# Cross attention: four PSUM banks shared in one ring, and quadrant swaps written as a maximum

## The reference, cut to what matters

```
q = (query @ Wq + bq).reshape(B, L, NKV, G, HDIM)      # 512 -> 32 heads of 128
k_, v_ = split(kv @ Wkv + bkv, 2, axis=-1)             # 512 -> 8 + 8 heads of 128
scores = einsum('blkgd,bmkd->bkglm', q, k) * scale
attn = softmax(scores, axis=-1)
o = einsum('bkglm,bmkd->blkgd', attn, v).reshape(B, L, NHEAD * HDIM)
return o @ Wo + bo
x = _layernorm(x + that)
```

## Time and profile before

| | |
|---|---|
| three runs | 2900.38 us median (2898.84 to 2906.28) |
| the profiled execution | 2909.86 us, its span on the core 2908.0 us |
| busy over the span | PE 2756.5 (95%), PEld 2389.1 (82%), DVE 1962.4 (67%), ACT 1461.6 (50%), POOL 1595.9 (55%) |
| chain that ended last | PE 84%, DVE 10%, issue 2%, POOL 2%, ACT 2%, DMA 1% |
| mean granted clock of TensorE | 0.984 |
| first scores of cross attention read by DVE | 1651.82 us |
| scores of step 60 read by DVE | 2750.49 us |

### The profile page before, as it was taken

The page is one execution under the profiler, slowest core; times in us unless marked ns, Lnnn a source line. Parts: engine busy times, 40 slices in busy tenths (PEclk is TensorE's granted clock), DMA queues, the critical chain, the costliest instruction groups (busy, mean ns, idle before and its releaser), DMA issues.

```text
span 2908.0 us, 63698 instructions
## 1 busy us (share of the span) xinstructions
PE 2756.5 (95%) x26368; PEld 2389.1 (82%) x26368; DVE 1962.4 (67%) x3893; ACT 1461.6 (50%) x3079; POOL 1595.9 (55%) x1363
## 2 busy tenths in 40 slices
PE   7999999999999999999999999989898989899977
PEld 6889888888888888888888877777787777777766
DVE  6666666666676666666666676756566777565777
ACT  6566666666666666555666333423233343332335
POOL 6888888888676666666667422323233323232225
PEclk9999999999999999999999999999999999999999
DMA  5323323331352123222322210101011111111101
GB/s 174 92 66 102 106 73 89 102 105 54 106 165 81 56 79 86 71 68 79 86 65 77 75 54 19 55 19 55 19 57 46 40 33 40 33 40 33 30 30 58
DMA packets 91481, 197.68 MB, mean 68 GB/s; under 512 B 20664, under 2 KB 21304, under 8 KB 89144
## 3 DMA queue, kind: packets, MB, share of 16 engines
q1 hardware_dynamic: 71480, 154.80, 18.6%
q10 hardware_dynamic: 17664, 34.61, 3.5%
q0 software_dynamic: 2048, 4.20, 0.5%
HBM read 176.78 MB, written 16.78 MB: 67 GB/s over the span
## 4 chain that ended last, share of the span: by engine, by line
PE 84%; DVE 10%; issue 2%; POOL 2%; ACT 2%; DMA 1%; SPq 0%; ACTq 0%; DVEq 0%
PE big L1813 28%; PE bank L1813 27%; PE big L1885 14%; PE bank L1905 12%; PE big L1905 3%; DVE xol L1470 2%; DVE P L1643 2%; DVE mxo L1632 1%; DVE mx L1645 1%; DVE P L1651 1%; DMA raw<-in_xWo 1%; DVE xvl L1461 1%; DVE nmx L1374 0%; POOL xwol L512 0%; DVE P L1380 0%
## 5 line engine op out<-in xcount | busy, mean ns | idle before, releaser
L777 POOL TENSOR_TENSOR ptl<-P,pth 128x576 fp32r<-128x576 f32 x512 | 724.9, 1435 | 241.6 <-ACT pth L953 241.0
L944 ACT ACTIVATE P<-big,nmx 128x576 f32<-128x576 f32 x512 | 378.5, 739 | 405.8 <-DVE nmx L1374 405.5
L1380 DVE STREAM_TRANSPOSE P<-P 128x576 f32<-128x576 f32 x512 | 387.7, 767 | 149.9 <-ACT P L944 147.6
L1905 PE MATMUL bank<-pth,v 32*128 32x256 f32 x4608 | 423.7, 280 | 4.6 <-DVE xacc L1402 1.5
L1905 PE MATMUL big<-pth,v 32*128 32x256 f32 x4608 | 423.8, 281 | 0.0
L853 POOL TENSOR_TENSOR P<-P,sm 128x512 f32<-128x512 f32 x64 | 67.2, 1050 | 616.9 <-DVE sm L1666 616.9
L1905 PEld LDWEIGHTS bank<-pth,v 32*128 32x128 f32 x4608 | 383.7, 187 | 16.9 <-issue 14.3
L1374 DVE TENSOR_REDUCE nmx<-big 128x1 f32<-128x576 f32 x512 | 373.1, 746 | 5.0 <-PE big L1885 3.0
L953 ACT ACTIVATE pth<-P 128x576 fp32r<-128x576 f32 x512 | 347.7, 682 | 51.8 <-DVE P L1380 51.4
L1905 PEld LDWEIGHTS big<-pth,v 32*128 32x128 f32 x4608 | 362.8, 187 | 0.0
L1905 PE MATMUL bank<-ptl,v 32*128 32x256 f32 x2304 | 351.1, 278 | 0.0
(11 more groups left out here) (265 smaller groups left out, 7687.1 us busy)
## 6 DMA issues: line engine op xcount, KB each, us to landing
rall<-kept_r ACTq DMA_DIRECT2D x64, 512.0 KB, 3.6
raw<-in_wo SPq DMA_DIRECT2D x64, 256.0 KB, 3.3
raw<-in_xWq SPq DMA_DIRECT2D x64, 256.0 KB, 2.7
raw<-in_xWo SPq DMA_DIRECT2D x64, 256.0 KB, 2.7
raw<-in_wq SPq DMA_DIRECT2D x62, 256.0 KB, 2.8
v<-kept_v SPq DMA_DIRECT2D x24, 448.0 KB
v<-kept_v SPq DMA_DIRECT2D x68, 128.0 KB, 3.3
raw<-in_xWkv SPq DMA_DIRECT2D x32, 256.0 KB, 2.7
```

The source lines that it names most:

```text
L777: pool.tensor_tensor(third_columns(ptl, i), blocks_of(i), f(third_columns(pth, i)), ALU.subtract).then_inc(p_low(i), 1)
L944: act.activation(P[:, i % PSLOTS, :].rearrange("p (k n) -> p k n", k=2), ps_s[i % 2][:, :, 0:HALF], ACT.Exp, bias=nmx[:, i % 8:i % 8 + 1], ...
L1380: dve.transpose(P[:, i % PSLOTS, :], P[:, i % PSLOTS, :]).then_inc(p_turned(i), 1)
L1905: m = pe.matmul(ps_o[a][:, 0:256], v[r, s, l, :], p[r, lo:hi + 1:hi - lo, block_of(b), :, :], start=first, stop=final)
```

## The change

The ring has four banks, 0 to 3, and the two projections of a step take their turns in it as well. Tiles `x3` from number 8 on, which come after the last step, still alternate between banks 0 and 1. The order in which PE, DVE, ACT and POOL do their work stays as it is; what each use of a bank waits for moves. `swap_halves` is four `tensor_tensor` maxima of a quadrant with itself instead of four `tensor_copy`.

```
+RING = 4
+
...
-        ps_w = [bank[1][:, :], bank[0][:, :]]
...
-                at[key] = q_banks[turn % 2]
+                at[key] = q_banks[turn % (RING if key[0] != "x3" or key[1] < HT else 2)]
...
-                for tt in early_x3(n):
-                    put(("x3", tt))
-                if n == 0:
-                    put(("k", 0, 3))
+                if n == STEPS - 1:
+                    for tt in early_x3(n):
+                        put(("x3", tt))
+                if n >= 1:
+                    put(("w", n - 1, 0))
+                    put(("w", n - 1, 1))
+                if n < STEPS - 1:
+                    for tt in early_x3(n):
+                        put(("x3", tt))
...
+            put(("w", STEPS - 1, 0))
+            put(("w", STEPS - 1, 1))
...
-                dve.tensor_tensor(xa(tt), ps_w[i], xa(tt), ALU.add).then_inc(acc_done((2, n, i)), 1)
+                dve.tensor_tensor(xa(tt), bank_at[("w", n, i)], xa(tt), ALU.add).then_inc(acc_done((2, n, i)), 1)
...
-                    dve.tensor_copy(dst[32 * a:32 * a + 32, :], src[32 * b:32 * b + 32, :]).then_inc(signal(event), 1)
+                    of = src[32 * b:32 * b + 32, :]
+                    dve.tensor_tensor(dst[32 * a:32 * a + 32, :], of, of, ALU.max).then_inc(signal(event), 1)
...
-                    b = ring[0] % 2
+                    b = ring[0] % (RING if key[0] != "x3" or key[1] < HT else 2)
...
-                ps = ps_w[i]
-                bank_free(3 - i, (acc_done, (2, n, i)))
+                ps = q_bank(("w", n, i), (acc_done, (2, n, i)))
...
-                    gate.wait_ge(acc_done, (2, STEPS - 1, 1))
+                    if q == 1:
+                        bank_free(2)
...
-            bank_free(3)
...
+                if tt == 2:
+                    bank_free(3)
```

More of the change, by code:

```diff
@@ L1298, in bank_order @@
                 if n == 0:
+                    put(("k", 0, 3))
                     put(("v", 0, 3))
```

## The result

The changed kernel takes 2814.35 us (median of four runs, 2813.18 to 2815.67), the kernel before 2901.01 us in the same comparison: the ratio is 0.9699, with a 95% interval of 0.9682 to 0.9716. That is 86.7 us less; 92.6 were forecast. The profiled execution took 2814.78 us with a span of 2813.0, against 2909.86 and 2908.0 before, so between the two profiled executions the difference is 95.0 us.

What follows compares the result with a forecast made beforehand. PE's waits for `xvl` in cross attention's odd steps were taken as the bound. Terms 64.9 + 9.5 + 16.8 + 3.1 - 1.7 = 92.6 us, off the median 2900.4, gave 2807.8 us; range 2794 to 2845.

Steps and rivals of the forecast that it cites:

- "issue" waits: Seven PE waits at even groups' starts, 14.4 us, with DVE held by the projection weights' split; predicted to stay.
- The first term: In odd groups' steps of cross attention, all 28 PE waits for `xvl` go: 64.9 us.
- The second term: Twelve matmuls behind each `xvl` wait take 3.06 us instead of 2.72; 0.34 x 28 gives 9.5 us.
- The third term: PE's granted clock, below full in five of seven odd groups, becomes full: 16.8 us, bounds 0 and 16.8.
- The fourth term: In step 0, PE's wait for `xql` before a key goes: 3.1 us.
- Step 29: DVE, held by the projection weights, begins late; a new PE wait for `xol` takes back 1.7 us.
- The margin: In odd steps, DVE finishes `xol` 1.15 us before PE reaches the first projection.
- The maximum: In `swap_halves`, each maximum takes 9 ns more than a copy and is stopped by POOL alike; counted as 0.
- A: In odd groups the clock does not come back: gain 75.8 us, time 2824.6 us; chance 0.2.
- B: The wait moves to the projection, for `xol`, taking back half: gain 46 us, time 2854 us; chance 0.14.
- C: Maxima between scores and `xol` are dear, so the kernel is slower: loss 181 us, time 2989 us; chance 0.03.
- D: The ring frees nothing because the following use of a bank holds PE: time 2900 us; chance 0.03.

## Why the prediction was right, point by point

**The mechanism** was right in each part. The 28 waits for `xvl` are gone, the queries do not wait for the additions nor the projections for key and values, the "issue" waits stayed, and the size of each term held roughly. The time, 2814.35, is 6.5 us above the forecast.

**The first term**, 64.9 us, came off whole. The experiment with the values first shows that it is the time at which the value bank is read that counts: with two banks, and the bank free 1.41 us earlier, it gave half.

**The second term**, the restart, was misread, though its sum with the first was right. The 3.06 us are a piece of the chain; by the starts of the matmuls the twelve behind the wait take 2.90:

```profile
1933.99 0.50 PE L1813 MATMUL big<-yTh,wqTh 128*128 128x512 f32 x1 [2.14 <-DVE xvl L1461]
...
1936.89 0.39 PE L1813 MATMUL bank<-xwoh,xoh 128*128 128x512 f32 x1
```

The restart is 0.18 us and not 0.34. The 0.16 that are missing belong to the wait, since the view counts 2.14 from the modelled end of the matmul before, which lies that much behind the time at which the next one would have started. The two errors cancel: 2.14 + 0.34 = 2.48, and a plain odd step fell from 20.23 to 17.75. That is 0.08 more than the 17.67 reckoned, because the values' 24 matmuls take 2.88 us in the chain and not 2.80; over 28 steps it is 2 us.

**The third term**, the clock, was the mis-sized one. "I take all of it; the bounds are 0 and 16.8": between the two profiled executions all 16.8 came by that reckoning, since the odd groups are now at 1.00 throughout, and that is why the difference there, 95.0 us, is no smaller than the sum. But 16.8 was what one execution of the kernel before had lost. Others with the same waits lost 8.5 and 13.5, and the prediction put the sum against the median of the runs, where it did not belong in full. It had noted that the profiled execution was 9.5 us slower than that median and found no row for it; the clock rows account for most of it. A term that differs between executions should be taken at a typical size, or the sum made for the profiled execution alone: 2909.9 - 92.6 = 2817.3 against 2814.8 measured. With the 8.5 us of the execution that took 2899.6, close to the median, the sum is 84.3 and the forecast 2816.1, 1.8 above the measured median.

**The fourth term**, step 0: 3.1 us were forecast, and group 0 is 5.0 us shorter. Most of the rest is the clock, which the term left out: group 0 was at 0.95 before and is at 0.97 after, by missing share times length 3.4 and 1.9 us, and the repeated kernel before, with the same wait of 3.1 us, had it at 0.97 and took 66.6 us instead of 68.1. About 0.4 us are left for the restart.

**Step 29**: 1.7 us were to come back; PE waited 1.0 us before the tile transposes, and group 7 is 1.5 us longer than in the versions without that wait (76.1 against 74.6).

**The margin** of 1.15 us was 0.91, and 0.8 of added work is hidden. PE reaches the projection 6.41 us after DVE's head, not 6.52, and the sum left out the 0.13 us between the end of `xol` and the matmul that waits for it (1906.04 to 1906.17 in the kernel with the maxima three times). The rest, from 0.91 to 0.8, is the slower twelve matmuls behind a stop. None of it touched the time, since DVE was inside 0.8 as well.

**The maximum**: 9 ns more each were allowed, with 0 in the sum. It is the copy to the nanosecond. That it would be stopped by POOL like the copy was right: its longest is 1211 ns like the copy's, and beside POOL's split of `xT` four take 1.79 us like the copies.

The rivals fell by one row each: A by the clock of 1.00 in the odd groups, B by the plain steps' 17.75 us, C by the maximum's 167 ns, D by the list of waits, in which neither `xacc` nor `xk` nor `xvl` stands.

## What to carry to other kernels

When an engine waits for a buffer, look at which reader frees it and what that reader does first in its own order: moving the reader or rotating more buffers are two ways to the same end, and here the order alone gave half and three banks nearly all. Count as gain not only the wait but the slow restart and the low clock behind it, take all lengths from start to start, and take the clock from more than one execution. When a stall goes, measure how far the next one is (here 0.8 us), by adding work rather than from a sum of pieces, and look for the engine that is held in its order by a piece of work it need not do: handing one block's low part to POOL was worth a third of the whole change.

## What the runs showed of the hardware

A maximum of a 32 x 16 quadrant with itself, both inputs in SBUF, takes the same time as a copy: minimum 161, median 167 ns, and at most 1211 ns. In the changed kernel four of them took more than 0.9 us together in two places only, 1.79 us at 2693.15 and 1.88 at 2713.14, and both lie beside POOL's splits (2690.79 to 2694.52, and from 2710.83 on). Twelve matmuls of 512 columns take 2.72 us in a stream, 2.90 behind a wait of 2.1 us and 2.84 behind one of 0.5, with the granted clock at 1.00 in all these stretches. They also take 2.89 with no wait (1885.98 to 1888.87 in the changed kernel), behind the small matmuls of the attention output. The granted clock of PE in the same places differs between executions of one program whose waits agree to 0.4 us: it was 0.96 in group 1 in one execution of the kernel before and 1.00 in the other, and 0.96 and 1.00 in group 13. In the kernel with no waits of PE in the steps (the norms moved) it was 1.00 in all 15 groups, and in the kernel before with only the edit for POOL 0.98 in each of the seven odd ones. What decides between these values was not tested.
